# A short list of sources for the gathers of cycle 0, and a fourth group that gathers rows of x

## The chip, the core and the metric

The kernel runs on one core of a Trainium2 chip. The metric is the time of one execution in device microseconds (us). The engines are named as in the profile: PE (TensorE, the matrix engine; PEld is its weight load), DVE (VectorE), ACT (ScalarE), POOL (GpSimd) and SP (SyncE, which here only issues DMAs). ACT issues DMAs too, and POOL issues the indirect ones, the gathers. L12 is line 12 of the kernel.

## What is computed

A graph network layer with a residual and a layer norm over 3125 nodes of 128 features and 53125 edges, sorted by destination.

```python
h   = concatenate([x[row], edge_attr], axis=1)            # 53125 x (128 + 64)
h   = relu(batch_norm(h @ W1 + b1, g1, be1))
s   = segment_sum(h, col, num_segments=n)
agg = where(cnt > 0, s / maximum(cnt, 1.0), 0.0)
h2  = relu(batch_norm(concatenate([x, agg], axis=1) @ W2 + b2, g2, be2))
out = layer_norm(x + relu(h2 @ Wl + bl))
```

## The kernel before

**Tiling.** The edges are padded to 104 groups of 512 (four tiles of 128 edges). Four groups (q = 0 to 3) make one of 26 cycles i; group number g = 4i + q. The product of a group is the sum of an edge part, edge_attr times the lower rows of W1, and a node part, x[src] times the upper rows of W1.

**Node part.** In most groups the node part comes from a table ytab in DRAM, which holds x @ W1 for all nodes. PE computes it first (L751, seven batches, from x_turned), ACT copies it out of PSUM (L1006), SP writes it to DRAM (L507), and POOL gathers 512 of its rows a group, one indirect DMA for 128 rows (`gather`, L670 to 684). From cycle 1 on, three of the four tiles of group q = 2 don't come by a gather: PE picks their rows with one-hot matrices (`pick`, L783) that DVE (L1320) and ACT (L1096, L1099) build, so that 13 gathers a cycle are left. A second copy of the table, split in a high part (ACT, L1012) and a low part (DVE, L1247), is kept in SBUF for that.

**Cycle 0.** ytab isn't ready when the edge work could begin. So the first EARLY = 3 groups of cycle 0 gather rows of x itself (`gather_x`, L661 to 666). PE turns such a group (four transposes, `turn_first`, L810) into a PSUM bank, psC[0] or psC[1] by turns, ACT copies it out (`x_rows_out`, L1027), and PE adds its product with W1 (L827) to the edge part (`product_first`, L822). The fourth group gathers from ytab like all later ones, and DVE adds what it gathered to the edge part (L1307). The order on PE is: turn 0, turn 1, product 0, turn 2, product 1, product 2, product 3, counts, products 4 and 5, then the picks of cycle 1.

**Startup.** ACT issues its DMAs at L997 to L1001 in this order: g1 spread, src (the source numbers of all 104 groups, 208 KB), the upper W1, the destination rows, the destinations. POOL waits for src, then issues the 12 gathers of x in order; ahead of the third group it waits for the last batch of the table (L689), and ahead of the ytab gathers for the written table and for the semaphore s_idx (L691, L692). SP waits for the upper W1 (L475) between its second and third load of x_turned.

**Order on DVE.** It prepares signs and indices (up to L1270, which raises s_idx), takes the last five low parts (L1247), makes the one-hots of cycle 0 (`onehots`, L1285), presets psS and psX (L1386, L1387), and then in each cycle for q = 0 to 3: make_h (in cycle 0 L1295 for a group with rows of x, L1307 otherwise), sum_h (L1328), the sum of the squares of the group before (L1335), and for q = 0 the one-hots of the next cycle. After cycle 0 it copies two constants to PSUM (L1365, L1366) and builds the first node one-hots (L1320).

**Lead of the gathers.** From group 4 on, `gather` waits for h_ready of g - 3: POOL can be at most four groups ahead of DVE.

The bank psC[1] is also batch 2 of the table (psY[2]) and the bank of product 2 (psP[2]). PE therefore waits before turn 1 until the low part of that batch is taken (s_low, L806).

Of the kernel before, what the change touches and what calls it, by code (L numbers as in the profile page):

```python
# [28 lines left out]
I32 = mybir.dt.int32  # L29
F32R = mybir.dt.float32r  # L30
ALU = mybir.AluOpType
ACT = mybir.ActivationFunctionType
AX_X = mybir.AxisListType.X

P = 128
EPS = 1e-5
TINY = 1e-20
TILES = 4
# [3 lines left out]
WIN = 64  # L42
BEYOND = 64
WIDE = 256
EARLY = 3
QUAD = 32
NODE0 = 1
NODEQ = 2
# [5 lines left out]
    return PICKED if i >= NODE0 else 0  # L54


def gnn_kernel(nc, E, x, xt, src, src_rows, dst, dst_rows, ea, W1, b1, g1, be1, W2, b2, g2, be2, Wl, bl, out):
    N, F = x.shape
    NI, FE = ea.shape[0], ea.shape[1] // 2
    H2 = W2.shape[1] // P  # L60
# [2 lines left out]
    NG = NI * U  # L63
# [12 lines left out]
    BATCH = [(t, min(4, NT - t)) for t in range(0, NT, 4)]  # L76
# [10 lines left out]
    with ctx:  # L87
        def sb(name, shape, dt=F32):
            return ctx.enter_context(nc.sbuf_tensor(name, shape, dt))
# [4 lines left out]
        def sem(name):  # L94
            return ctx.enter_context(nc.semaphore(name))
# [26 lines left out]
        hotb2 = work[:, 5, :].bitcast(BF16).rearrange("p (q w) -> p q w", q=U)  # L122
        agg = sb("agg", [P, NAGG])
        cnt = sb("cnt", [P, NAGG])
        srci = sb("srci", [P, TILES, NG], I32)
        loc = sb("loc", [P, TILES, NG])
        basei = sb("basei", [1, NG], I32)
        ident = sb("ident", [P, P])
        w1x = sb("w1x", [P, F])
# [91 lines left out]
        psC = [pb(f"psC{i}", [P, GF]) for i in range(2)]  # L221
        psS = pb("psS", [P, 512])
        psX = pb("psX", [P, 512])
        psA = [psH[0], psH[1], psC[0], psC[1]]
        psP = [psH[0], psH[1], psC[1]]
        psY = [psH[0], psH[1], psC[1], psS, psX]
        PARTS = [0, 1, 5, 6, 2, 3, 4]
        assert sorted(PARTS) == list(range(len(BATCH)))
# [36 lines left out]
        s_w1x = sem("w1x_loaded")  # L265
        s_w = sem("w_loaded")
        s_rows = sem("dst_loaded")
        s_src = sem("src_loaded")
        s_node = sem("node_numbers_ready")
        rows_in = [sem(f"src_rows_spread{k}") for k in range(2)]  # L270
# [107 lines left out]
        def slot(i, par, q):  # L378

            return resg(i, q) if q < KEEP else away[par][:, (q - KEEP) * GF:(q - KEEP + 1) * GF]  # L380
# [263 lines left out]
        @block.gpsimd  # L644
        def _(pool):
            pool.memset(ident[:, :], 0.0).then_inc(s_pool, 1)
            pool.wait_ge(s_pool, 1)
            pool.affine_select(out=ident[:, :], in_=ident[:, :], compare_op=ALU.not_equal, fill=1.0, base=0,
                               pattern=[[-1, P]], channel_multiplier=1).then_inc(s_ident, 1)
            pool.memset(zeros, 0.0).then_inc(s_zr, 1)  # L650
            pool.iota(iota[:, :], [[1, WIN]], base=0, channel_multiplier=0,
                      allow_small_or_imprecise_dtypes=True)
            pool.iota(nodeid, [[1, NT]], base=0, channel_multiplier=NT,
                      allow_small_or_imprecise_dtypes=True).then_inc(s_node, 1)
            pool.memset(onesb[:, :], 1.0)
            pool.memset(onesf, 1.0).then_inc(s_onesf, 1)
            pool.memset(ones[:, :], 1.0)
            pool.memset(epsc[:, :], EPS)
            pool.drain().then_inc(s_set, 1)

            def gather_x(q):  # L661

                rows = slot(0, 0, q)
                for j in range(TILES):
                    pool.indirect_dma_start(
                        rows[:, j * F:(j + 1) * F], None, x,
                        bass.IndirectOffsetOnAxis(ap=srci[:, j, q:q + 1], axis=0)
                    ).then_inc(x_gathered[q], 16)

            def gather(i, q):  # L670

                g = U * i + q
                if g >= U:
                    pool.wait_ge(h_ready, g - 3)
                if i >= 2 and q == KEEP:
                    pool.wait_ge(spilled[i % 2], 16 * (i // 2))
                if (i + 1) * KEEP * GF > XT0 and q == 0:
                    pool.wait_ge(x_ps, len(XSTEPS))
                rows = slot(i, i % 2, q)
                for j in range(node_tiles(i) if q == NODEQ else 0, TILES):  # L680
                    pool.indirect_dma_start(  # L681
                        rows[:, j * F:(j + 1) * F], None, ytab,
                        bass.IndirectOffsetOnAxis(ap=srci[:, j, g:g + 1], axis=0)
                    ).then_inc(gathered[i % 2][q], 16)

            pool.wait_ge(s_src, 16)
            for q in range(EARLY):
                if q == EARLY - 1:
                    pool.wait_ge(s_yps, len(BATCH))  # L689
                gather_x(q)  # L690
            pool.wait_ge(s_tab, TAB)  # L691
            pool.wait_ge(s_idx, 1)  # L692
            for i in range(NI):
                for q in range(EARLY if i == 0 else 0, U):
                    gather(i, q)

            def add_window(i, q):

                g = U * i + q
                base = nc.values_load(basei[0:1, bass.ds(g, 1)], engines=(mybir.EngineType.Pool,), min_val=0,  # L700
                                      max_val=N, skip_runtime_bounds_check_because="dst holds node numbers")
                pool.wait_ge(wsum_ready, g + 1)
                if not first(i, q, 1):
                    pool.wait_ge(agg_added, g)
                w = agg[:, bass.ds(base, WIN)]
                pool.tensor_tensor(w, w, wsum[:, q, :], ALU.add).then_inc(agg_added, 1)  # L706

            pool.wait_ge(s_wide, 1)
            wide = pool.value_load(rowi[0:1, 0:1], min_val=0, max_val=N)

            with pool.If(wide < WIN):
                pool.wait_ge(agg_set, 3)
                for i in range(2):
                    for q in range(U):
                        add_window(i, q)
                with pool.Fori(1, NI // 2) as k:
                    for i in (2 * k, 2 * k + 1):
                        for q in range(U):
                            add_window(i, q)
                pool.wait_ge(agg_added, NG)  # L720
                pool.sem_inc(sums_over, 1)

            pool.wait_ge(sums_over, 1)
            pool.wait_ge(s_rcb, 16 * RCP)
            for c0, cw in CHUNKS[DVE_MEAN:]:
                pool.tensor_tensor(agg[:, c0:c0 + cw], agg[:, c0:c0 + cw], cnt[:, c0:c0 + cw], ALU.mult
                                   ).then_inc(s_meanp, 1)
# [3 lines left out]
        def _(pe):  # L731
# [69 lines left out]
            def turn_first(q):  # L801

                if q < EARLY:
                    pe.wait_ge(x_gathered[q], 64)
                    if q == 1:
                        pe.wait_ge(s_low, PARTS.index(2) + 1)  # L806
                    if q >= 2:
                        pe.wait_ge(xg_copied, q - 1)
                    for j in range(TILES):
                        last = pe.transpose(psC[q % 2][:, j * P:(j + 1) * P], slot(0, 0, q)[:, j * F:(j + 1) * F],  # L810
                                            ident[:, :])
                    last.then_inc(xg_turned, 1)

            def product_first(q):

                if q == 0:
                    pe.wait_ge(ea_loaded[0], 16)
                    pe.wait_ge(s_low, PARTS.index(6) + 1)
                if q >= len(psP):
                    pe.wait_ge(h_ready, q - len(psP) + 1)  # L820
                for b in range(2):
                    last = pe.matmul(psP[q % len(psP)][:, b * 2 * F:(b + 1) * 2 * F], ea_cols(0, q, b),  # L822
                                     w1e[:, :, :].rearrange("p a f -> p (a f)"), start=(b == 0), stop=(q >= EARLY and b == 1))
                if q < EARLY:
                    pe.wait_ge(xg_copied, q + 1)
                    for j in range(TILES):
                        last = pe.matmul(psP[q % len(psP)][:, j * F:(j + 1) * F], xgt[q % 2][:, j * P:(j + 1) * P], w1x[:, :],  # L827
                                         start=False, stop=(j == TILES - 1))
                last.then_inc(prod_ready, 1)
# [164 lines left out]

        @block.scalar
        def _(act):
            act.dma_start(gbc, g1.partition_broadcast(P)).then_inc(s_w1x, 16)  # L997
            act.dma_start(srci[:, :, :], src).then_inc(s_src, 16)
            act.dma_start(w1x[:, :], W1[0:F, :]).then_inc(s_w1x, 16)
            act.dma_start(drow[0:NG, :].bitcast(I32), dst_rows).then_inc(s_rows, 16)  # L1000
            act.dma_start(dsti.bitcast(I32).rearrange("p (j g) -> p j g", j=TILES), dst).then_inc(s_rows, 16)  # L1001
            def table_out(b):
# [19 lines left out]
            def x_rows_out(q):  # L1022

                act.wait_ge(xg_turned, q + 1)
                if q >= 2:
                    act.wait_ge(prod_ready, q - 1)
                act.activation(xgt[q % 2], psC[q % 2][:, :], ACT.Copy).then_inc(xg_copied, 1)  # L1027

            def squares(i, q):

# [588 lines left out]
```

## Time and profile before

| | |
|---|---|
| median of 3 runs | 587.01 us (585.83 to 587.88) |
| the profiled execution, its own time | 587.13 us |
| its span in the profile | 585.4 us |
| granted clock of PE over the span | 0.982 |
| PE busy | 526.8 us, 90% |
| DVE busy | 508.8 us, 87% |
| ACT busy | 421.7 us, 72% |
| POOL busy | 363.2 us, 62% |

The profile is of one execution. Its span leaves out 1.73 us of that execution's time. Busy shares are means over stages with different limits; which wait ends last is read stage by stage. A timeline's rows give the start in us, the duration in us, engine, line, operation, out<-in, shapes and count, and in brackets the idle time of the engine before the row with what ended it.

### The profile page before, as it was taken

What the parts mean: (1) busy time and instruction counts of PE and PEld (TensorE: products, weight loads), DVE (VectorE), ACT (ScalarE), POOL (GpSimd) and SP (SyncE); (2) the same over time, 40 slices, a digit from 0 to 9 for tenths busy, and PEclk for the clock granted to TensorE, in tenths of its full rate; (3) what the DMA queues carried; (4) which work ended last, traced back from release to release, by engine and by line L of the source; (5) the groups of instructions that cost most, each with busy time, mean ns of one, the idle gap of its engine ahead of it and who ended that gap; (6) DMA issues with size and microseconds to landing.
All of it is one profiled execution on the core that took longest, in us unless ns stands there. A gap on an engine that the chain in (4) does not pass through costs nothing.

```text
span 585.4 us, 10554 instructions
## 1 busy us (share of the span) xinstructions
PE 526.8 (90%) x3117; PEld 463.1 (79%) x3117; DVE 508.8 (87%) x719; ACT 421.7 (72%) x850; POOL 363.2 (62%) x464
## 2 busy tenths in 40 slices
PE   4679999999999999999999988888998999999993
PEld 4557878877777878888888877776877999999683
DVE  5796999999999999999999999998976877777787
ACT  3458877787778877888888887777767655655476
POOL 4776777777777777777777777777770333333500
PEclk9779999999999999999999999999999999999997
DMA  7744554445544555444444444444345789886004
GB/s 201 253 157 141 170 173 150 143 158 176 171 157 141 170 175 164 150 154 154 147 151 150 144 154 157 157 133 143 108 141 180 269 273 300 288 283 181 2 1 111
DMA packets 48140, 97.02 MB, mean 166 GB/s; under 512 B 10886, under 2 KB 23605, under 8 KB 48100
## 3 DMA queue, kind: packets, MB, share of 16 engines
q1 hardware_dynamic: 30734, 63.38, 32.7%
q0 software_dynamic: 10912, 22.37, 13.8%
q10 hardware_dynamic: 6453, 10.79, 5.0%
q8 instruction: 19, 0.31, 0.2%
q14 instruction: 22, 0.17, 0.1%
HBM read 70.11 MB, written 26.37 MB: 165 GB/s over the span
## 4 chain that ended last, share of the span: by engine, by line
PE 58%; DVE 13%; POOL 8%; issue 7%; DMA 7%; ACT 6%; ACTq 0%; DVEq 0%; POOLq 0%
PE psT L783 26%; PE psH L925 7%; PE psC L925 6%; POOL res L681 6%; PE psH L765 5%; PE psT L846 4%; DMA res<-ytab,srci 3%; PE psC L765 3%; DVE node_hot L1320 2%; ACT node_hot L1096 2%; DVE psX L1335 2%; PE psH L792 1%; ACT node_rows_turned L1086 1%; ACT node_hot L1099 1%; PE psT L838 1%
## 5 line engine op out<-in xcount | busy, mean ns | idle before, releaser
L681 POOL DMA_INDIRECT res<-ytab,srci x265 | 250.1, 944 | 81.8 <-issue 75.9
L783 PE MATMUL psT<-node_hot,node_table 125*128 125x384 f32 x1250 | 260.7, 357 | 5.1 <-DVE node_hot L1320 4.6
L783 PEld LDWEIGHTS psT<-node_hot,node_table 125*128 125x128 f32 x1250 | 220.8, 190 | 30.0 <-issue 12.8
L1320 DVE TENSOR_TENSOR node_hot<-agg,psC 125x1920 fp32r<-125x1920 int32 x75 | 160.9, 2147 | 0.0
L1096 ACT ACTIVATE node_hot<-agg,nodeid 125x384 fp32r<-125x384 int32 x250 | 131.7, 603 | 6.6 <-PE psT L783 4.5
L1099 ACT ACTIVATE node_hot<-node_hot,ones 125x1920 fp32r<-125x1920 f32 x50 | 95.1, 1902 | 1.6
L1436 DVE TENSOR_TENSOR work<-res,psX 128x512 f32<-128x512 f32 x104 | 70.7, 687 | 21.8 <-PE psH L925 11.7
L706 POOL TENSOR_TENSOR agg<-agg,srci 128x64 f32 x104 | 32.0, 308 | 76.6 <-ACT srci L1162 73.8
L765 PE MATMUL psH<-w1e,work 128*128 128x256 f32 x268 | 70.5, 385 | 6.8 <-DVE work L1305 3.0
L681 POOL DMA_INDIRECT work<-ytab,srci x64 | 62.1, 970 | 21.7 <-issue 17.1
L1335 DVE TENSOR_TENSOR psX<-agg,psX 128x512 f32<-128x512 f32 x103 | 71.1, 690 | 4.5 <-ACT agg L1033 4.5
L765 PEld LDWEIGHTS psH<-w1e,work 128*128 128x128 f32 x268 | 47.6, 189 | 16.8 <-DVE work L1305 6.7
L1033 ACT ACTIVATE agg<-res 128x512 f32<-128x512 f32 x77 | 47.5, 618 | 14.1 <-DVE res L1307 7.3
L1328 DVE TENSOR_TENSOR psS<-res,psS 128x512 f32<-128x512 f32 x77 | 53.6, 696 | 2.6
L925 PE MATMUL psH<-work 128*128 128x128 f32 (+1 forms) x416 | 51.1, 276 | 3.1 <-DVE work L1436 1.5
L925 PEld LDWEIGHTS psH<-work 128*128 128x128 f32 x416 | 48.5, 192 | 4.0 <-ACT srci L1162 2.8
L925 PE MATMUL psC<-work 128*128 128x128 f32 (+1 forms) x416 | 50.7, 275 | 0.0
L925 PEld LDWEIGHTS psC<-work 128*128 128x128 f32 x416 | 48.5, 192 | 0.0
L765 PE MATMUL psC<-w1e,work 128*128 128x256 f32 x132 | 34.8, 386 | 3.3 <-DVE res L1305 1.6
L1061 ACT ACTIVATE cnt<-psT 1x64 f32 x104 | 22.4, 215 | 21.3 <-PE psT L838 18.6
L765 PEld LDWEIGHTS psC<-w1e,work 128*128 128x128 f32 x132 | 23.4, 189 | 8.6 <-DVE res L1305 3.4
L1307 DVE TENSOR_TENSOR res<-psH,res 128x512 f32<-128x512 f32 x42 | 28.7, 683 | 1.5 <-DMA res<-ytab,srci 1.2
(222 smaller groups left out, 536.4 us busy)
## 6 DMA issues: line engine op xcount, KB each, us to landing
work<-in_edge_attr SPq DMA_DIRECT2D x26, 512.0 KB, 3.4
res<-spill SPq DMA_DIRECT2D x25, 512.0 KB, 4.2
spill<-work SPq DMA_DIRECT2D x13, 512.0 KB, 2.7
spill<-res SPq DMA_DIRECT2D x12, 512.0 KB, 2.7
agg<-in_src_rows SPq DMA_DIRECT2D x25, 192.0 KB, 3.9
res<-ytab,srci POOLq DMA_INDIRECT x265, 2.5
hot_dram<-hotb ACTq DMA_DIRECT2D x13, 256.0 KB, 3.1
hot_dram<-work ACTq DMA_DIRECT2D x13, 256.0 KB, 3.1
```

The lines of the kernel that those rows point to most:

```text
L681: pool.indirect_dma_start(rows[:, j * F:(j + 1) * F], None, ytab, bass.IndirectOffsetOnAxis(ap=srci[:, j, g:g + 1], axis=0)).then_inc(gath ...
L706: pool.tensor_tensor(w, w, wsum[:, q, :], ALU.add).then_inc(agg_added, 1)
L765: last = pe.matmul(psP[g % len(psP)][:, b * 2 * F:(b + 1) * 2 * F], ea_cols(par, q, b), w1e[:, :, :].rearrange("p a f -> p (a f)"), start= ...
L783: last = pe.matmul(rows_at, table[0:PN, part, (t0 + t) * F:(t0 + t + 1) * F], hot_now[0:PN, t, :], start=(n == 0 and t == 0 and part == 0) ...
L925: last = pe.matmul(psA[q][:, 0:n], mx[:, q, j * F:(j + 1) * F], hotf[:, q, j * WIN:j * WIN + n], start=(j == 0), stop=(j == TILES - 1))
L1033: act.activation(sq[g % 2], slot(i, i % 2, q), ACT.Square).then_inc(sq_ready, 1)
L1096: act.activation(hots[2][0:PN, t, :], rows[i % 2][0:PN, :].bitcast(I32), ACT.Abs, bias=nodeid[0:PN, t0 + t:t0 + t + 1], scale=-1.0).then_i ...
L1099: act.activation(hots[2][0:PN, :, :], hots[2][0:PN, :, :], ACT.Relu, bias=ones[0:PN, :], scale=-1.0).then_inc(hot_by_act, 1)
L1320: dve.tensor_tensor(dve_hot(i, d)[0:PN, :, :], rows[i % 2][0:PN, :].bitcast(I32).unsqueeze(1).broadcast_to([PN, CUT, HOTW]), nodep[:, t0:t ...
L1328: last = dve.tensor_tensor(psS[:, :], slot(i, par, q), psS[:, :], ALU.add)
L1335: last = dve.tensor_tensor(psX[:, :], sq[g % 2], psX[:, :], ALU.add)
L1436: dve.tensor_tensor(tiles(mx[:, q, :]), tiles(hin), negu, ALU.max).then_inc(m_ready, 1)
```

## The change

- A new input src_first holds the source numbers of the four groups of cycle 0 alone (128 partitions x 4 tiles x 4 groups of int32, 64 bytes a partition, 8 KB). ACT issues its load first of all its DMAs, and the load of src moves behind that of the upper W1.
- EARLY goes from 3 to 4: all 16 gathers of cycle 0 take rows of x, by the short list. POOL waits for the short list, issues them without the wait for the last batch, and only then waits for src, and for the written table.
- The fourth group so gets four transposes, an ACT copy and four more tile products on PE (L810, L1027, L827 of before), and its make_h on DVE becomes a copy.
- The turned rows go to psC[0] and psT[0] by turns. The wait of PE for the low part of batch 2 moves from turn 1 to product 2.

```diff
-EARLY = 3
+EARLY = 4
...
+        srcf = sb("srcf", [P, TILES, EARLY], I32)
...
+        psTurn = [psC[0], psT[0]]
...
-                        bass.IndirectOffsetOnAxis(ap=srci[:, j, q:q + 1], axis=0)
+                        bass.IndirectOffsetOnAxis(ap=srcf[:, j, q:q + 1], axis=0)
                     ).then_inc(x_gathered[q], 16)
...
+            pool.wait_ge(s_srcf, 16)
+            for q in range(EARLY):
+                gather_x(q)
             pool.wait_ge(s_src, 16)
-            for q in range(EARLY):
-                if q == EARLY - 1:
-                    pool.wait_ge(s_yps, len(BATCH))
-                gather_x(q)
             pool.wait_ge(s_tab, TAB)
...
                     pe.wait_ge(x_gathered[q], 64)
-                    if q == 1:
-                        pe.wait_ge(s_low, PARTS.index(2) + 1)
                     if q >= 2:
                         pe.wait_ge(xg_copied, q - 1)
                     for j in range(TILES):
-                        last = pe.transpose(psC[q % 2][:, j * P:(j + 1) * P], slot(0, 0, q)[:, j * F:(j + 1) * F],
+                        last = pe.transpose(psTurn[q % 2][:, j * P:(j + 1) * P], slot(0, 0, q)[:, j * F:(j + 1) * F],
...
+                if q == 2:
+                    pe.wait_ge(s_low, PARTS.index(2) + 1)
...
+            act.dma_start(srcf[:, :, :], src_first).then_inc(s_srcf, 16)
             act.dma_start(gbc, g1.partition_broadcast(P)).then_inc(s_w1x, 16)
+            act.dma_start(w1x[:, :], W1[0:F, :]).then_inc(s_w1x, 16)
             act.dma_start(srci[:, :, :], src).then_inc(s_src, 16)
-            act.dma_start(w1x[:, :], W1[0:F, :]).then_inc(s_w1x, 16)
...
-                act.activation(xgt[q % 2], psC[q % 2][:, :], ACT.Copy).then_inc(xg_copied, 1)
+                act.activation(xgt[q % 2], psTurn[q % 2][:, :], ACT.Copy).then_inc(xg_copied, 1)
```

## Rows read from the trace of the kernel before

**Rows 1.** Chain of waits, 0 to 48 us: start us, duration us, what.

```profile
16.71 5.36 DMA res<-in_x,srci
...
34.78 2.16 DVE node_hot L1320
...
37.08 3.54 PE psT L783 x10
...
42.48 1.85 PE psT L783 x10
```

**Rows 2.** Waits, POOL 56 to 300 us, DVE whole span: total us, times, longest.

```profile
POOL work L681 <- DVE res L1307: 4.0, 7, 1.3
...
DVE res L1307 <- DMA res<-ytab,srci: 7.8, 7, 2.0
```

**Rows 3.** DMA issues, 0 to 6 us: count, KB each, median us from issue to landing.

```profile
srci<-in_src ACTq DMA_DIRECT2D x1, 208.0 KB, 6.2
...
res<-in_L_gnn_g ACTq DMA_DIRECT2D x1, 64.0 KB, 4.9
w1x<-in_L_gnn_W ACTq DMA_DIRECT2D x1, 64.0 KB, 6.0
```

**Rows 4.** Timeline of POOL: gathers of cycle 0, the first of cycle 1.

```profile
7.77 1.14 POOL L665 DMA_INDIRECT res<-in_x,srci  x1 [5.47 <-DMA srci<-in_src]
...
21.71 0.94 POOL L665 DMA_INDIRECT work<-in_x,srci  x1 [0.30 <-issue]
23.22 1.70 POOL L681 DMA_INDIRECT work<-ytab,srci  x1 [0.57 <-DMA ytab<-res]
...
27.72 1.86 POOL L681 DMA_INDIRECT work<-ytab,srci  x1 [0.30 <-issue]
29.89 0.94 POOL L681 DMA_INDIRECT res<-ytab,srci  x1 [0.30 <-issue]
```

**Rows 5.** Landing of gathers: line 665 (all 12), then line 681 from 24 to 60 us.

```profile
DMA to landing us min/median/max: 3.4/4.3/5.4
...
DMA to landing us min/median/max: 2.4/2.5/4.2
```

**Rows 6.** Timeline of DVE, 16 to 33 us.

```profile
16.02 0.49 DVE L1254 TENSOR_TENSOR w1e<-w1e,res 128x128 f32<-128x128 f32 x2 [1.91 <-DMA col<-in_L_gnn_b]
...
22.90 1.20 DVE L1285 TENSOR_TENSOR hotb<-iota,loc 128x1024 bf16<-128x1024 f32 x1
...
26.22 0.69 DVE L1295 COPY res<-psH 128x512 f32<-128x512 f32 x1 [0.99 <-PE psH L827]
...
27.55 1.22 DVE L1285 TENSOR_TENSOR work<-iota,loc 128x1024 bf16<-128x1024 f32 x1
...
30.60 0.68 DVE L1295 COPY work<-psC 128x512 f32<-128x512 f32 x1
...
32.52 0.68 DVE L1307 TENSOR_TENSOR work<-psH,work 128x512 f32<-128x512 f32 x1
```

**Rows 7.** Timeline of PE, 19 to 37 us.

```profile
19.58 1.12 PE L810 MATMUL psC<-ident,res 128*128 128x128 f32 x4 [3.29 <-DVE col L1270]
22.12 1.12 PE L810 MATMUL psC<-ident,res 128*128 128x128 f32 x4 [1.43 <-DMA res<-in_x,srci]
...
26.02 0.60 PE L810 MATMUL psC<-ident,work 128*128 128x128 f32 x4
...
27.32 1.05 PE L827 MATMUL psH<-w1x,res 128*128 128x128 f32 x8
...
32.13 1.03 PE L765 MATMUL psC<-w1e,work 128*128 128x256 f32 x4
```

**Rows 8.** Windows of PE: stretch, width, busy (count), granted clock, DMA share, GB/s.

```profile
16.20:19.50 3.30, 0.10 (x1) 0.88 0.99 386
...
25.00:26.00 1.00, 1.00 (x8) 0.73 0.97 334
```

**Rows 9.** Timeline of ACT: the first node one-hots of ACT end.

```profile
39.59 1.90 ACT L1099 ACTIVATE node_hot<-node_hot,ones 125x1920 fp32r<-125x1920 f32 x1
```

More of the change, by code:

```diff
@@ L54, in node_tiles, with gnn_kernel @@
     return PICKED if i >= NODE0 else 0
-def gnn_kernel(nc, E, x, xt, src, src_rows, dst, dst_rows, ea, W1, b1, g1, be1, W2, b2, g2, be2, Wl, bl, out):
+def gnn_kernel(nc, E, x, xt, src_first, src, src_rows, dst, dst_rows, ea, W1, b1, g1, be1, W2, b2, g2, be2, Wl, bl, out):
     N, F = x.shape
@@ L267, in gnn_kernel @@
         s_rows = sem("dst_loaded")
+        s_srcf = sem("first_src_loaded")
         s_src = sem("src_loaded")
@@ L1601 @@
         'x_turned': x.reshape(N // NT, NT, F).transpose(2, 1, 0),
+        'src_first': src.reshape(NG, P, TILES)[0:EARLY].transpose(1, 2, 0),
         'src': src.reshape(NG, P, TILES).transpose(1, 2, 0),
```

## The prediction

> **What bounds the kernel now.** I read the page's busy shares first, then the chain of waits, then the timelines of the first 45 us, since the change touches nothing later. PE is the busiest engine, and from 37.08 us on the chain runs mostly over its picks [rows 1]. Before that it runs through the startup: the load of src, eight gathers on POOL, the landing of the eighth (16.71 + 5.36 = 22.07 us), PE's turn 1 and product 0, then DVE, which ends in the first node one-hots (34.78 us) and lets PE start pick 0 at 37.08 [rows 1, 4, 6]. What the change is worth is how far it moves that handover to the steady cycles. I take as the mark the second pick of cycle 1, which starts at 42.48 [rows 1]: from there on PE has no gap that the startup could fill or open.
>
> Is the shift of the mark passed on whole? The gathers take about 1.25 us each, POOL is held back by h_ready again and again until some 250 us [rows 2], and from about 320 us on DVE waits for gathers instead [rows 2]. So POOL's pace sets a late stretch, but its place in it was tied to DVE before. An earlier POOL alone is given back at these waits; an earlier DVE and PE is kept. I count the mark's shift one to one.
>
> **When the short list lands.** Nothing in the trace is an 8 KB load at the start of the queue. The nearest row is the g1 spread, which is first on ACT's queue now, with the same 128 packets of 512 bytes: 4.9 us [rows 3], and POOL starts 0.28 us after its list has landed, by the present case (1.26 + 6.2 = 7.49 against 7.77). That gives 0.81 + 4.9 + 0.3 = 6.0 us. From below, the fastest landing of any gather is 2.4 us [rows 5], which gives 3.5; from above, the 6.0 us of the upper W1 [rows 3] gives 7.1. I take 5.7, close to the g1 row, because the packets carry an eighth of its bytes: POOL starts 2.1 us earlier.
>
> The Trainium skill (DMA: Bandwidth & Descriptors, Specifications) says that transfers under 512 bytes a descriptor fall below line rate, since the engine then reads, modifies and writes. The packets of the short list are 64 bytes. No row here times such packets at this place; were each to cost twice a 512-byte one, the list would land later than the g1 row and POOL would start nearer to 6.3 than to 5.7, by an estimate from that rule.
>
> **The gathers.** Twelve starts span 21.71 - 7.77 = 13.94 us [rows 4], so the sixteenth starts 13.94 + 4 x 1.25 = 18.9 us after the first. Two gathers of now are stretched from 0.94 to 1.70 and 1.86 us, and both began within 0.4 us after DVE began one-hots (22.90 and 27.55 us) [rows 4, 6]; those one-hots will now meet gathers 13 to 16. I take one stretch, 0.9 us; ends 0 and 2.0. Landing from start was 3.4 us at best and 4.3 in the middle for rows of x, 2.5 in the middle later, with less traffic [rows 5]; the sixteenth falls between these, so 3.4. The fourth group is then in SBUF at T = 5.7 + 18.9 + 0.9 + 3.4 = 28.9 us, between 26.9 and 31.
>
> **What goes.** Turn 1 no longer waits until 22.12 [rows 7]: the eighth gather lands by about 20, and the bank's wait moves to product 2, where the low part (done near 21.8) is long past. Turn 0 still waits for s_idx at 19.5. Product 0 then ends near 24 instead of 26.2, before DVE is free; DVE's 0.99 us of idle time ahead of the first make_h [rows 6] goes. The upper W1 behind 8 KB instead of 208 KB lands up to 1 us earlier (it is 6.0 us now [rows 3]), which starts the table and, through SP's wait, the small loads for which DVE waits at 16.02 [rows 6] up to that much earlier; I take 0.7. Left alone, DVE would so be 0.99 + 0.7 = 1.7 us ahead, more where the node one-hots gain too. The load of src now ends later, by perhaps 0.5 us, but nothing needs it before gather 17. The wait for the last batch (L689) never held POOL. The 1.70 and 1.86 us gathers and the 0.57 us wait for the table go from before gather 17, which starts near 26.6 instead of 29.89 [rows 4]: worth nothing by itself, see above.
>
> **What comes.** Turn 3 stands on PE ahead of product 2, so products 2 and 3, the counts, products 4 and 5 and the first pick are queued behind the landing at T. Now product 2 waits for no gather of ytab. With PE at its full clock a turn and a product take 28.37 - 26.02 = 2.35 us [rows 7], so DVE's make_h of group 2 can start at T + 2.3 = 31.2; it is at 30.60 now [rows 6]. So DVE's lead of 1.7 us is lost, 0.6 more with it. Make_h of group 3 follows 1.92 us behind, as now (32.52 - 30.60) [rows 6]: product 3 takes about 1.8 us on PE and just keeps up. The ACT copy of the fourth group (0.6 us) hides beside product 2; had it no cover it would cost its 0.6. The DVE copy costs 0.68 as the sum does now.
>
> **The mark.** Behind make_h of group 3 two paths lead to the mark. On ACT the node one-hots end 41.49 - 32.52 = 8.97 us later [rows 6, 9]. On PE the first pick starts 37.08 - 32.52 = 4.56 us later, takes 3.54 at the low clock, and x_product brings it to 42.48 [rows 1]. PE is last now, 1.0 us behind ACT. The low clock came from the gap of PE between 33.2 (end of product 5 [rows 7]) and 37.08. With the change PE is busy until T + 6.4 and its first pick comes at T + 8.8: a gap of 2.4 instead of 3.9 us, short enough, I think, to stay at the high clock; a pick then takes 1.8. So ACT's path ends last: the mark is at T + 2.3 + 1.92 + 8.97 + 0.1 = T + 13.3 = 42.2 against 42.48, 0.3 us earlier.
>
> **Sum.** 587.13 - 0.3 = 586.8 us, against the profiled execution's own time, which lies 0.12 above the median of the three runs.
>
> **The rivals.**
> 1. PE is cold at turn 3 (ends slower). Product 1 ends near 25.7, and PE is then idle until T, 3.2 us. Its clock fell in a gap of 3.3 us now (16.2 to 19.5, mean 0.88 falling to the low level of 0.50, 1.2 GHz) and rose 3.4 us after work had begun again at 22.12 [rows 7, 8]. Cold, turn and product take what turn 1 and product 0 take now, 26.22 - 22.12 = 4.1 us [rows 6, 7], 1.8 more. The mark is then at T + 15.1 = 44.0: 588.6 us; with T at 29.6 it is 589.3. It decides from the length of PE's gap before turn 3. The Trainium skill (TensorE: Matmul & The Clock Gate, Part 1) gives the same two levels, and says that the moment of a switch varies from run to run against the kernel's work; by that rule the case is a coin's toss rather than settled, and the traces so far show only gaps of 3.3 us or more that ended cold.
> 2. The list lands early, by 4 us or so, with no stretched gather. T is then under 27.4, DVE never waits for turn 3, and its lead of 1.7 us and ACT's 1.0 us of slack are both taken: about 2.6 us, 584.5.
> 3. POOL's lead counts. Gather 17 starts 3.3 us earlier; were the h_ready waits no real tie, the late stretch that waits for gathers [rows 2] would end that much earlier: 583.8. Against it stand the waits themselves, which recur every cycle.
> 4. It does nothing it says: the list lands no earlier than src does now, T is above 30 and the end is later than in rival 1, 589.5 to 590. The landing rows of the first loads speak against it [rows 3].
>
> **How the numbers follow.** Forecast (PE warm at turn 3, T between 27.5 and 29.5: 585.4 to 587.4): 0.45. Rival 1: 0.32, of which a third is over 588.9. Rival 2: 0.15. Rival 3: 0.03. Rival 4: 0.05. The range leaves out rival 3 and most of rival 4: 584.4 to 589.4, and the likeliest case's own range is 585.4 to 587.4. A difference of 0.3%, 1.76 us, is about what a measurement of this kernel can tell from none. Faster by more: rivals 2 and 3 and a little of the forecast's lower end, 0.2. Slower by more: the late third of rival 1, rival 4, and a little for what I don't see, 0.2. Within: 0.6.
>
> **What would show it.** POOL's first gather near 5.7 us; the sixteenth starting near 25.5, with one gather longer than 0.94 beside one-hots of DVE; turn 1 right behind turn 0; PE idle before turn 3 and released by a gather of x; DVE waiting for PE ahead of its third make_h; the first pick at 1.8 us instead of 3.54; the second near 42.2. Steps are wrong if turn 3 finds its rows landed, if DVE has no wait there, or if cycles after the mark take other than now. The prediction as a whole is wrong if the list lands outside 4.8 to 6.3 us, or if POOL's place in the late stretch moves by other than the mark.

## The result, and the profile after

| | before | changed |
|---|---|---|
| median of 16 runs each, us | 587.70 (585.30 to 588.97) | 589.63 (588.16 to 591.50) |
| profiled execution: span / own time, us | 585.4 / 587.13 | 588.7 / 590.46 |

The changed kernel is slower by about a third of a percent: ratio 1.0034, interval 1.0018 to 1.0051. (The ratios here are estimated from all executions and aren't exactly the quotients of the medians.) The forecast was 586.8 with a range of 584.4 to 589.4. Against the profiled execution of before, the own time rose by 3.33 us.

The profile page of the changed kernel: span, busy shares, and the chain's share by engine.

```profile
span 588.7 us, 10581 instructions
...
PE 530.6 (90%) x3129; PEld 467.1 (79%) x3129; DVE 509.2 (86%) x719; ACT 422.3 (72%) x851; POOL 362.7 (62%) x464
...
PE 41%; POOL 23%; DVE 14%; issue 13%; DMA 5%; ACT 2%; DVEq 0%; ACTq 0%; POOLq 0%
```

PE is still the busiest engine. The startup tells more. The chain of waits of the changed kernel, 0 to 48 us, against [rows 1] (start us, duration us, what):

```profile
0.80 3.05 DMA srcf<-in_src_first
...
4.13 1.14 POOL res L668
...
23.27 6.03 DMA work<-in_x,srcf
29.30 0.04 issue
29.34 0.85 PE psT L810 x4
30.20 1.71 PE psC L824 x4
31.90 1.52 PE psC L829 x8
...
37.64 2.16 DVE node_hot L1323
39.80 0.14 issue
39.94 3.52 PE psT L785 x10
43.46 1.87 PE psT L848 x2
45.34 1.77 PE psT L785 x10
```

The chain now goes through the first load of ACT, the whole list of 16 gathers, the landing of the last one (6.03 us), and PE's turn 3 at 29.34. The mark, the second pick of cycle 1, is at 45.34 where it was at 42.48: 2.86 us later.

DMA issues of the changed kernel, 0 to 6 us, against [rows 3], and 21 to 24 us (count, KB each, median us to landing):

```profile
res<-in_L_gnn_g ACTq DMA_DIRECT2D x1, 64.0 KB, 3.9
w1x<-in_L_gnn_W ACTq DMA_DIRECT2D x1, 64.0 KB, 4.4
...
srcf<-in_src_first ACTq DMA_DIRECT2D x1, 8.0 KB, 3.1
```

```profile
agg<-in_src_rows SPq DMA_DIRECT2D x2, 192.0 KB, 6.1
```

Timeline of DVE in the changed kernel (start us, busy us, what, idle time before it and its releaser), against [rows 6]: the first, third and fourth make_h of cycle 0.

```profile
23.19 0.66 DVE L1298 COPY res<-psH 128x512 f32<-128x512 f32 x1
...
33.45 0.69 DVE L1298 COPY work<-psC 128x512 f32<-128x512 f32 x1 [5.81 <-PE psC L829]
...
35.38 0.68 DVE L1298 COPY work<-psH 128x512 f32<-128x512 f32 x1
```

Timeline of PE, and windows of PE (stretch, width, busy and count, granted clock, DMA share, GB/s), against [rows 7, 8]:

```profile
18.84 0.66 PE L810 MATMUL psT<-ident,res 128*128 128x128 f32 x4 [0.56 <-DMA res<-in_x,srcf]
19.36 1.99 PE L824 MATMUL psH<-w1e,work 128*128 128x256 f32 x4
...
29.34 0.85 PE L810 MATMUL psT<-ident,work 128*128 128x128 f32 x4 [4.13 <-DMA work<-in_x,srcf]
29.99 1.92 PE L824 MATMUL psC<-w1e,work 128*128 128x256 f32 x4
```

```profile
28.00:29.00 1.00, 0.00 (x0) 1.00 0.28 86
29.00:30.00 1.00, 0.66 (x5) 0.83 0.24 66
30.00:31.00 1.00, 1.00 (x4) 0.50 0.05 12
...
33.00:34.00 1.00, 1.00 (x7) 0.96 0.25 66
```

DVE's first make_h is at 23.19 instead of 26.22, 3.03 us ahead. Then it waits 5.81 us for product 2, because PE stood 4.13 us before turn 3 and then worked at the low clock for some three microseconds. (I call PE warm at the granted clock 1.00, which is 2.4 GHz, and cold at 0.50, 1.2 GHz.) The windows show the fall late: 1.00 is still granted in the idle slice from 28 to 29 us, and the mean of 0.83 from 29 to 30 puts the fall behind the start of turn 3. So turn 3 takes 0.85 us, between the 0.66 of a warm turn and the 1.12 of a cold one [rows 7], and the cold clock costs most in product 2. The whole lead goes and 2.85 us more: the third make_h is at 33.45 instead of 30.60.

To follow the shift I use one instruction that stands in each cycle, the ACT copy of the picked rows. I call it the marker; it is not the mark of the prediction, which is the second pick of cycle 1. Its timelines, first before, then changed, in cycle 1 and in cycle 25, the last one:

```profile
51.78 0.49 ACT L1086 ACTIVATE node_rows_turned<-psT 128x384 f32<-128x384 f32 x1 [0.79 <-PE psT L783]
...
434.70 0.49 ACT L1086 ACTIVATE node_rows_turned<-psT 128x384 f32<-128x384 f32 x1 [0.79 <-PE psT L783]
```

```profile
54.57 0.49 ACT L1089 ACTIVATE node_rows_turned<-psT 128x384 f32<-128x384 f32 x1 [0.79 <-PE psT L785]
...
438.76 0.49 ACT L1089 ACTIVATE node_rows_turned<-psT 128x384 f32<-128x384 f32 x1 [0.78 <-PE psT L785]
```

The shift is 2.79 us in cycle 1 and 4.06 in cycle 25. So the cycles after the mark add 1.27 us, which the prediction had at zero. The own time rose by less than the marker, 3.33 us, since what follows the marker differs too: own time less the marker's start in cycle 25 is 152.43 us before and 151.70 changed, and 150.23 to 153.69 over all fourteen traces of this document. A single execution's time says little of a shift below 2 us; the marker says more. Two stalls are new in them, shown with the last group of experiments.

### The profile page after: what moved, and what is told of

Same layout as the page of the kernel before. It is cut to its first block, busy times and chain, and to the rows that moved or that the text cites. A ratio compares the mean times of both kernels' runs of the same rounds, so it can differ in the third digit from the quotient of the medians.

```text
span 588.7 us, 10581 instructions
## 1 busy us (share of the span) xinstructions
PE 530.6 (90%) x3129; PEld 467.1 (79%) x3129; DVE 509.2 (86%) x719; ACT 422.3 (72%) x851; POOL 362.7 (62%) x464
## 4 chain that ended last, share of the span: by engine, by line
PE 41%; POOL 23%; DVE 14%; issue 13%; DMA 5%; ACT 2%; DVEq 0%; ACTq 0%; POOLq 0%
POOL res L684 18%; PE psT L785 14%; PE psH L927 7%; PE psC L927 7%; PE psH L767 3%; DMA res<-ytab,srci 3%; DVE node_hot L1323 3%; PE psT L848 3%; POOL work L684 2%; DVE psX L1338 2%; POOL res L668 1%; PE psC L767 1%; DVE res L1474 1%; PE psH L794 1%; POOL work L668 1%
## 5 line engine op out<-in xcount | busy, mean ns | idle before, releaser
L684 POOL DMA_INDIRECT work<-ytab,srci x60 | 56.6, 944 | 26.0 <-issue 16.1
```

Source lines behind the costliest of these rows:

```text
L684: pool.indirect_dma_start(rows[:, j * F:(j + 1) * F], None, ytab, bass.IndirectOffsetOnAxis(ap=srci[:, j, g:g + 1], axis=0)).then_inc(gath ...
```

## The experiments

Two theories at the start. **A**: the loss is turn 3 standing on PE ahead of ready work, made larger by the low clock; the short list itself is a gain. **B**, the rival: the short list or the new order of the loads costs something itself. A second question was how large the clock's part is, and what makes gather 16 land 6.03 us after its start.

**Three groups again, with the short list.** The changed kernel, with:

```diff
-EARLY = 4
+EARLY = 3
```

> The changed kernel with EARLY back at 3: short list first, src behind the upper W1, the turned rows in psC[0] and psT[0], the low-part wait at product 2, but the fourth group gathers from ytab again. Theory A (the fourth group's turn stands on PE ahead of product 2, waits there for gather 16, and PE has lost its clock by then): without turn 3 DVE's third make_h comes near 27.6 us instead of 33.45 (30.60 before), the fourth near 30 (32.52 before), and the kernel is 2 to 3 us faster than before, 584.7 to 585.7 against 587.7. Rival B (the short list, the order of loads or the banks cost the time): as slow as the changed kernel, 589 to 590. Rival C (POOL's lead or a random stall of POOL in the later cycles makes the difference): no better than before, within 1 us of 587.7.

Measured: 585.75 us against 587.26 beside it, ratio 0.9969 (0.9956 to 0.9983). Timeline of DVE (third make_h) and of PE (first pick) in this kernel:

```profile
28.66 0.68 DVE L1298 COPY work<-psC 128x512 f32<-128x512 f32 x1
```

```profile
35.14 3.54 PE L785 MATMUL psT<-node_hot,node_table 125*128 125x384 f32 x10 [4.21 <-DVE node_hot L1323]
```

DVE waits for nothing ahead of its third make_h, which is 1.94 us ahead of [rows 6], and the marker is ahead by 1.92 us in cycle 1 and 1.75 in cycle 25. The 1.5 us between the medians are less than the 2 to 3 that I expected (the third make_h came at 28.66, not near 27.6), but that one line of the change, the fourth group, is the whole loss.

**The list alone.** The same, with the old banks and waits back, so that the kernel before differs by the list and the order of the loads only:

```diff
+            act.dma_start(srcf[:, :, :], src_first).then_inc(s_srcf, 16)
             act.dma_start(gbc, g1.partition_broadcast(P)).then_inc(s_w1x, 16)
+            act.dma_start(w1x[:, :], W1[0:F, :]).then_inc(s_w1x, 16)
             act.dma_start(srci[:, :, :], src).then_inc(s_src, 16)
-            act.dma_start(w1x[:, :], W1[0:F, :]).then_inc(s_w1x, 16)
```

> The kernel before with the short list and the new order of the loads alone: 12 gathers of x by the list, old banks and both old waits. Theory A: PE's turn 1 waits for the low part of batch 2 near 19.8 us, product 0 ends near 24.2, a microsecond later than with the new bank, and DVE is so 1.5 to 2 us ahead of before: 585.7 to 586.2. Rival B, if the list or the order of loads costs the time: 589 or more. If only the new bank brings DVE ahead: same as before, 587.7.

Measured: 585.86 us against 587.26, ratio 0.9981 (0.9965 to 0.9998); the marker is ahead by 2.12 and 1.81 us. That is the last kernel's gain. The other bank and the moved wait bring nothing that these runs show, and theory B has fallen: the list and the load order together are a gain of some 1.5 us (1.51 and 1.40 between the medians). No run parts the list from the order of the loads.

**The loads of cycle 1 held back.** SP issues 512 KB and 2 x 192 KB just ahead of gather 16. Here they wait for the fourth group:

```diff
+            sp.wait_ge(x_gathered[EARLY - 1], 64)
             load_ea(1, 1)
```

> The changed kernel, but SP holds its loads for cycle 1 (the second edge_attr tile, 512 KB, and two src_rows loads) until all four gathers of the fourth group have landed. In the changed kernel those loads were issued from 21.9 to 23.3 us, took 6 us each, and gather 16 (23.27 us) took 6.0 us too. If they crowd gather 16: it lands 3.4 to 4 us after its start, near 27, PE's gap before turn 3 is under 2.5 us and its clock stays up, the third make_h comes near 29.3, and the kernel is 3 to 4 us faster than the changed one, 585.5 to 586.5. If gather 16 is late for another reason (the small loads before it, POOL's next gather): it still lands at 29.3 and the time stays at 589 to 590, or rises by the later loads.

Measured: 587.49 us, ratio 0.9997 (0.9980 to 1.0014). Chain of waits, then the timeline of PE:

```profile
23.06 3.66 DMA work<-in_x,srcf
```

```profile
26.76 0.66 PE L811 MATMUL psT<-ident,work 128*128 128x128 f32 x4 [0.40 <-DMA work<-in_x,srcf]
...
35.70 1.97 PE L786 MATMUL psT<-node_hot,node_table 125*128 125x384 f32 x10 [2.60 <-DVE node_hot L1324]
...
40.64 2.94 PE L786 MATMUL psT<-node_hot,node_table 125*128 125x384 f32 x10 [1.09 <-ACT node_hot L1103]
```

Gather 16 lands in 3.66 us instead of 6.03, the third make_h is at 29.21, and pick 1 is warm at 1.97 us. But pick 2 waits 1.09 us for ACT's one-hots and runs cold, the marker ends only 0.08 us ahead of before in cycle 1, and by cycle 25 it is 1.09 late. So the time missed what I expected by a microsecond, though the landing and the third make_h came as expected. By an estimate from the medians, the crowding by SP's loads costs the changed kernel some 1.7 us (1.93 over the kernel before with it, 0.23 without; what holding the loads costs by itself is in that too). Without it the fourth group still only breaks even.

**PE kept busy in the gap.** Fourteen matmuls of the identity into an unused bank ahead of turn 3:

```diff
+                if q == EARLY - 1:
+                    for _ in range(14):
+                        pe.matmul(psT[1][:, 0:P], ident[:, :], ident[:, :], start=True, stop=True)
```

> The changed kernel with 14 products of the identity into an unused bank between product 1 and turn 3, about 3 us of PE work that nobody waits for. It leaves the landing of gather 16 as it is and keeps PE busy in the gap. Theory A with the clock as its second part: gather 16 lands near 29.3 as before, turn 3 and product 2 take 2.4 us instead of 4.1, and the kernel is 1.7 us faster than the changed one, about 588. If the clock has no part in the loss: no change from 589.6. If the filler itself delays turn 3: slower than 589.6.

Measured: 588.55 us, ratio 1.0026 (1.0010 to 1.0041). Timeline of PE:

```profile
24.43 3.29 PE L807 MATMUL psT<-ident 128*128 128x128 f32 x28
28.03 0.66 PE L813 MATMUL psT<-ident,work 128*128 128x128 f32 x4 [0.31 <-DMA work<-in_x,srcf]
28.52 1.03 PE L827 MATMUL psC<-w1e,work 128*128 128x256 f32 x4
...
42.11 3.14 PE L785 MATMUL psT<-node_hot,node_table 125*128 125x384 f32 x9 [1.29 <-ACT node_hot L1105]
```

Turn 3 and product 2 run at the high clock, the third make_h is at 30.48, before the place of [rows 6], and yet the marker is 1.38 us late: again pick 1 is warm, pick 2 waits for ACT and is cold. This run can't say that the filler was what kept the clock, since gather 16 landed by 28.0 here, and the next run is warm at that time without a filler.

**The changed kernel again, twice.** No edit; a single execution each, to see what varies.

> The changed kernel once more, for a second trace. Theory A: gather 16 lands 3.5 to 6 us after its start, turn 3 waits for it, DVE waits 3 to 6 us for its third make_h, and POOL's stall ahead of gather 130 is there again. If the first trace was a chance event: gather 16 lands under 27.5 us and DVE doesn't wait. Time 588.2 to 591.5.

> The changed kernel a third time, for the spread of gather 16's landing between executions: 26.8 to 29.5 us, with the second pick of cycle 1 moving by the same amount, and by 1.7 us more where PE's clock has fallen before turn 3. Time 588.2 to 591.5.

Measured: 588.11 and 590.38 us. Timeline of PE at turn 3 and window of PE from 29 to 30 us, for the first:

```profile
28.06 0.66 PE L810 MATMUL psT<-ident,work 128*128 128x128 f32 x4 [2.47 <-DMA work<-in_x,srcf]
```

```profile
29.00:30.00 1.00, 1.00 (x9) 1.00 0.24 61
```

The same two views for the second:

```profile
29.00 0.75 PE L810 MATMUL psT<-ident,work 128*128 128x128 f32 x4 [3.91 <-DMA work<-in_x,srcf]
```

```profile
29.00:30.00 1.00, 1.00 (x6) 0.72 0.27 66
```

The same program went either way. After a gap of 2.47 us PE was warm, the third make_h came at 30.51 and the marker 0.31 us early. After gaps of 3.91 and 4.13 it was cold, and the marker came 2.40 and 2.79 us late. The landing of gather 16 (4.71, 5.75 and 6.03 us) set how long PE stood. From that landing to the third make_h it was 2.50 us warm (30.51 - 28.01) and 4.16 and 4.15 cold, so the clock's part is 1.66 us, within one program.

SP's loads were issued at 20.67 us in the first of these, and at 21.89 and 21.94 in the others. That alone doesn't decide: in the four other traces with four groups whose loads weren't held (the filler and the three below with turn 3 behind) they were issued at 21.66 to 22.08, and gather 16 had landed by 27.84 to 28.31 us. With the loads held it landed at 26.72, without in all seven traces at 27.84 or later, up to 29.30. So the loads do delay it; why by 1 to 2.6 us, the runs don't show.

**Turn 3 behind product 2.** Product 2 needs no gather of the fourth group:

```diff
-                if q < U - 1:
+                if q < U - 2:
...
+                if q == U - 2:
+                    turn_first(q + 1)
```

> The changed kernel with one edit: PE does turn 3 behind product 2, not ahead of it. If PE's order is what exposes the late fourth group, the third make_h comes near 27.6 us (33.45 in the changed kernel), the fourth 2.5 us after gather 16's landing (4.2 us if PE has gone cold by then), so at 31 to 33 instead of 35.4, and the kernel is 2.5 to 4 us faster than the changed one at the second pick and 2 to 3 in time: 586.5 to 587.7. If the order is not it, and the landing alone decides (product 3 needs it in either order): the fourth make_h stays at 35 and the time near 589.6.

Measured: 587.01 us against 587.83, ratio 0.9995 (0.9972 to 1.0018). Timeline of DVE:

```profile
27.21 0.69 DVE L1300 COPY work<-psC 128x512 f32<-128x512 f32 x1
...
30.60 0.69 DVE L1300 COPY work<-psH 128x512 f32<-128x512 f32 x1 [1.37 <-PE psH L829]
```

The third make_h is 3.4 us early, the fourth 1.9, and so is the marker in cycle 1 (-1.90). Gather 16 had landed at 28.02, as in the warm execution of the changed kernel, whose marker was at -0.31: so PE's order alone is worth some 1.6 us there. The marker is now as early as with three groups, but in cycle 25 only 0.18 of it is left. Turn 3 was warm here (0.66 us at a granted clock of 1.00), so the late loss has nothing to do with the clock at turn 3.

**Three groups with one wait more.** To see whether the late loss comes from where instructions stand in POOL's stream, the three-group kernel got a redundant wait there:

```diff
             pool.wait_ge(s_src, 16)
+            pool.wait_ge(s_srcf, 16)
```

> The version with three groups of x (585.75 us) with one more wait on POOL, for a semaphore that has long been reached, ahead of the table's wait: it costs no waiting but moves all later instructions of POOL by one. In the three kernels with four groups POOL stood still for 1.5 us ahead of gather 130, near 176 us, which no kernel with three groups did. If that stall hangs on the place in POOL's instruction stream: it appears here too, ahead of gather 130, and the time is 0.4 to 1.0 us above the version with three groups. If it hangs on the fourth group's gathers themselves: no stall, 585.75 within the error.

Measured: 584.39 us against 587.83, ratio 0.9945 (0.9924 to 0.9965); the marker is ahead by 2.15 and 1.75 us. No late loss appears. The interval overlaps that of the first run with three groups, and both have the same 1.75 us in cycle 25, so I don't count the wait itself as a gain.

**Waits added on both engines.** Turn 3 behind product 2, with one redundant wait on POOL and one on DVE (which waits once less in cycle 0 when there are four groups):

```diff
+            pool.wait_ge(s_srcf, 16)
...
+                if i == 0 and q == U - 1:
+                    dve.wait_ge(s_set, 1)
```

> The version with turn 3 behind product 2 (587.01 us), with one wait more on POOL behind the x gathers and one more on DVE ahead of its fourth make_h, both for semaphores long reached. All kernels with four groups have two stalls that none with three has: DVE starts 0.35 us late in cycle 7 and POOL stands 1.5 us ahead of gather 130; together they are given about 1.5 us at the end of the edge pass. DVE has one wait fewer with four groups. If the stalls hang on places in the engines' instruction streams: DVE's goes (its stream has its old length again) or both move, and the time falls by up to 1.5 us to 585.5 to 586.5. If they hang on something else of the fourth group: both are where they were, 587.0.

Measured: 587.18 us against 587.13, ratio 0.9999 (0.9981 to 1.0018). Three kernels run for a single execution went with it: three groups with the list buffer and the semaphores made as for four, and both kinds with seven redundant waits on POOL.

> The version with three groups of x (585.75 us), but with the short list and the semaphores of four groups (16 bytes a partition more, one semaphore more that nobody waits for); the instructions are the same. If the two late stalls come from the layout of memory or semaphores: DVE's 0.35 us in cycle 7 and POOL's 1.5 us ahead of gather 130 appear here. If not: neither appears, and the picks start 1.9 to 2.1 us earlier than in the kernel before through all of cycles 1 to 18. Time 584.3 to 586.8.

> The version with turn 3 behind product 2 and the added wait on DVE, with seven waits for long reached semaphores on POOL behind the x gathers in place of one. One added wait left POOL's stall ahead of gather 130. If the stall hangs on a place in POOL's instruction stream that is coarser than one instruction: it moves to a gather a few places earlier, or goes. If it hangs on the gathers (their number, queue or targets): 1.5 us ahead of gather 130 again. DVE's stall in cycle 7 stays away in both cases. Time 585 to 589.

> The version with three groups of x with the same seven waits on POOL. Three groups have shown no stall with zero or one wait added. If a place in POOL's stream decides: one may appear here. If the fourth group's gathers decide: none. Time 584 to 587.

Measured: 586.30 us (beside 587.13), 586.82 and 585.78 (both beside 587.33). The gain of up to 1.5 us that I had put on both stalls going didn't come: only DVE's went. What matters is which show the two stalls. The first, in the timeline of DVE in cycle 7: before, changed, and with the wait added on DVE.

```profile
135.39 0.29 DVE L1304 TENSOR_TENSOR work<-psC,work 128x128 f32<-128x128 f32 x1 [1.14 <-PE psC L792]
```

```profile
138.69 0.29 DVE L1307 TENSOR_TENSOR work<-psC,work 128x128 f32<-128x128 f32 x1 [1.52 <-PE psC L794]
```

```profile
133.81 0.29 DVE L1312 TENSOR_TENSOR work<-psC,work 128x128 f32<-128x128 f32 x1 [1.17 <-PE psC L795]
```

DVE starts this sum 0.35 to 0.4 us late in every kernel with four groups, save the two with a wait added on DVE. Both of these had waits added on POOL too, so that it was DVE's that helped is likely but not shown. The marker's shift in the changed kernel goes from 2.95 us in cycle 6 to 3.35 in cycle 7. The second, in the timeline of POOL at gather 130: before, changed, turn 3 behind with waits added, three groups.

```profile
173.18 0.94 POOL L681 DMA_INDIRECT res<-ytab,srci  x1 [0.47 <-DVE work L1307]
```

```profile
177.86 0.94 POOL L684 DMA_INDIRECT res<-ytab,srci  x1 [1.81 <-issue]
```

```profile
172.98 0.94 POOL L684 DMA_INDIRECT res<-ytab,srci  x1 [1.81 <-issue]
```

```profile
171.43 0.94 POOL L684 DMA_INDIRECT res<-ytab,srci  x1 [0.48 <-DVE work L1310]
```

POOL stands 1.8 us ahead of its gather 130 and waits for nothing that the profile shows, in all eight traces of kernels with four groups and in none of the six with three (before among them). That is 1.5 us more than the 0.30 that POOL has ahead of most gathers. It stays with none, one or seven waits added on POOL, and doesn't come to three groups with these, nor with the wide buffer and four semaphores. So neither a shift of its place in POOL's stream by up to seven instructions nor the wider layout explains it. Its cause stays open.

What the second stall does can be followed, though. The shift of gather 300, in the late stretch, against that of the marker in cycle 25:

| kernel | gather 129 | gather 130 | gather 300 | marker, cycle 25 |
|---|---|---|---|---|
| changed | +3.34 | +4.68 | +4.01 | +4.06 |
| three groups | -1.76 | -1.75 | -1.74 | -1.75 |
| turn 3 behind | -1.34 | -0.05 | -0.32 | -0.18 |
| turn 3 behind, waits added | -1.55 | -0.20 | -0.89 | -0.88 |

The marker in cycle 25 stands within 0.14 us of gather 300 in these four, and 0.64 behind it in the filler kernel. So the late stretch goes by POOL's place, as the prediction said, in the main. In the kernel before, POOL waited for DVE longer than its usual 0.30 us four more times behind gather 130, the last at 238.79 us (0.48 us); in these three kernels with four groups it never does between gather 130 and 300.

## Why the prediction was wrong

The steps that failed are these: PE warm at turn 3 (1.8 us), a warm first pick (0.9 us), and nothing lost in the cycles behind the mark (1.3 us). The path was right: DVE waited for turn 3, as forecast. T, the time at which the fourth group has landed, came out 0.4 us off only because three wrong terms cancelled. In order:

**When the list lands: mis-sized.** 3.05 us and POOL at 4.13, where I had 4.9 or a little less and 5.7. The row I took, the g1 spread, had no fixed price: it landed in 4.9 us before [rows 3] and in 3.9 behind the short list. By the prediction's own test (4.8 to 6.3 us) this alone made the whole of it wrong. The Trainium skill (DMA: Bandwidth & Descriptors, Specifications) has descriptors under 512 bytes below line rate. Here 8 KB in 64-byte packets landed in 3.1 us, sooner than the 64 KB loads in 512-byte packets behind it (3.9 and 4.4), so no price of the rule shows at this size.

**The gathers: nearly right.** 23.27 - 4.13 = 19.1 us from the first start to the sixteenth; I had 18.9 and 0.9 more for one stretched gather, 19.8. The long one (1.89 us at 24.64) came just behind in this trace; in the filler kernel and with turn 3 behind product 2, gather 14 took 1.98 and 2.02 us.

**The landing of the sixteenth: mis-sized.** I took 3.4 us as there was "less traffic" later. It was 4.71, 5.75 and 6.03 us, and 3.66 with SP's loads held. Gather 16 now starts 1.3 us behind SP's first load for cycle 1, and I priced its landing without looking at SP's queue at that time. The errors cancelled: the list 1.6 and the gathers 0.7 us early, the landing 2.6 late, make T 29.3 in the first trace (28.0 and 29.0 in the other two), for a forecast of 28.9. That is luck.

**DVE's lead: mis-sized.** 3.03 us, not 1.7; the row of DVE's preparation that stood at 16.80 us (L1258) stands at 14.85 (L1261 of the changed kernel), 1.95 us earlier where I took 0.7. Turn 3 took all of it, as the prediction said, so this changed nothing here. It is what three groups keep (1.9 us).

**PE warm at turn 3: the choice that failed.** Two of three traces of the changed kernel are rival 1: PE idle 3.9 to 4.1 us, low clock, the third make_h T + 4.1 us (33.45 - 29.30), as it said. The one with a gap of 2.47 us is the forecast, T + 2.5. I gave the forecast 0.45 on a gap of 3.2 us, with only a row of 3.3 us that ended cold beside it [rows 8]: the nearest row spoke against the choice. That PE was idle up to T was right; that it kept its clock was not. The Trainium skill (TensorE: Matmul & The Clock Gate, Part 1) says that the moment of a switch varies from run to run against the kernel's work. The traces don't speak against it: turn 3 was warm behind a gap of 2.47 us, and of the eight first picks of kernels with four groups, behind gaps of 2.44 to 2.61 us, two kept the clock and six lost it. But these are six programs; within the changed kernel all three first picks went slow, so its traces don't show the variation for equal gaps.

**A warm first pick: failed.** I took 11.0 us from the third make_h to the mark instead of 11.88 before. I had thought a gap of 2.4 us short enough to keep the clock. In the eight traces with four groups the gap was 2.44 to 2.61 us; the pick took 1.97 us in two (loads held, filler) and 2.39 to 3.52 in six, where the clock fell during it. Measured for the 11.0: 11.89 (45.34 - 33.45) in the changed kernel's first trace and 11.72 (42.23 - 30.51) in the warm one. With the loads held the first pick was warm, the second waited for ACT and was cold (2.94 us), and it was 11.43 (40.64 - 29.21): ACT's path was 0.4 longer than I had it. The gain of 0.9 us on which the forecast's minus sign rested was nowhere; at best half of it.

**The mark passed on one to one: half right.** It held for three groups (-1.92 in cycle 1, -1.75 in cycle 25). With four it didn't: +0.4 us in cycle 7 and some 0.6 us behind gather 130, and the rest of the 1.27 in small steps. This term was in no part of the prediction. It is why even the warm execution (marker -0.31, then +1.07) took 588.11 us, and why the marker with turn 3 behind product 2 gains nothing in the end (-0.18, ratio 0.9995). With waits added it keeps 0.88 us, and still the ratio is 0.9999; the runs don't show where that goes, and a part may lie behind the marker.

Put together, from the forecast's T of 28.9: rival 1's cold turn (+1.8), a first pick that stays cold (+0.9), T later by 0.4, and the late loss (+1.3) make 4.4 us on top of the -0.3 forecast, +4.1 in all, for the marker's +4.06. In the runs' median it is less, +1.93. That some executions go the warm way, as one of three traces did, would lower it, but how many do isn't shown: the spread, 588.16 to 591.50, is no wider than that of the kernel before, 585.30 to 588.97.

**A version that beats both.** The short list with three groups: 585.75, 585.86 and 584.39 us in its three forms, ratios 0.9969, 0.9981 and 0.9945 to the kernel before, each interval below 1.

## What to carry to other kernels

A short first load for the first consumers, with the large one moved behind, was a gain by itself here; try it apart from any change that it makes possible. Don't put a step that waits for the last of a long list ahead of ready work on an engine that goes in order: its price here was the wait, the cold clock behind it, and the lead that the short list had won. And when a step is priced by a transfer, list what every other queue issues in the microseconds before it.

## What was not expected of the hardware

- Gather 16 landed in 3.66 us with SP's 896 KB of loads held back, and in 3.90 to 6.03 us in the seven traces where the first of them was issued 1.3 to 2.6 us before it started. A longer lead of the loads didn't order the landings: 1.33 us went with 6.03 and with 4.71.
- A DVE instruction in cycle 7 starts 0.35 to 0.4 us late, and not in the two kernels where one wait that holds nothing is added earlier in DVE's stream (with others on POOL). That it hangs on the place in the stream is a guess; why, the runs don't show.
- A stall of 1.8 us on POOL ahead of gather 130, in every kernel with four groups and none with three, with nothing in the profile that releases it. Not explained.
- The granted clock was still 1.00 at the end of a gap of 4.13 us and fell only once PE had begun again; in the six slow first picks, behind gaps of 2.44 to 2.61 us, it fell during the pick.
- With PE kept busy up to turn 3, the low clock came later: pick 1 ran warm and pick 2 cold, as it also did without a filler where the loads were held. In all fourteen traces pick 1 or pick 2 was slow.
